# First adapter weights loaded whole and picked on ScalarE, with TensorE's front in another order

## What is computed

```python
def L0(x, lang):                      # all of it per sequence
    h = relu(einsum('bsh,bha->bsa', x, W1[lang]) + b1[lang])      # W1 [10, 128, 32]
    y = x + einsum('bsa,bah->bsh', h, W2[lang]) + b2[lang]
    return layernorm(y) * gamma[lang] + beta[lang]
x = x + L0(x, lang)
# L1: three shared networks and two experts by kind, each relu(x @ wi) @ wo
# with wi [128, 512], wo [512, 128], mixed by a gate that reads token 0
x = x + L1(x, kind)
```

## Time and profile before

| | |
|---|---|
| median of 3 runs | 86.93 us (86.89 to 87.05) |
| the profiled execution | 86.88 us, of which its span is 85.1 |
| TensorE busy | 79.9 us |
| VectorE, ScalarE, GpSimd busy | 62.2, 49.4, 41.1 us |
| granted TensorE clock | 0.999 of full |
| DMA | 11998 packets, 7.49 MB |

### The profile page before, as it was taken

How to read it: one execution, slowest core, us unless ns; L and a number is a source line. 1 busy time by engine, 2 the same in 40 slices (tenths; PEclk the granted TensorE clock), 3 DMA queues, 4 the chain that set the end, 5 groups by cost and what they waited for, 6 DMA issues and landing times.

```text
span 85.1 us, 1653 instructions
## 1 busy us (share of the span) xinstructions
PE 79.9 (94%) x472; PEld 66.5 (78%) x472; DVE 62.2 (73%) x172; ACT 49.4 (58%) x116; POOL 41.1 (48%) x83
## 2 busy tenths in 40 slices
PE   4999999999999999999999899999999999999950
PEld 1377766886788898888999688888999898999820
DVE  4338769999799675446389995459777999389970
ACT  6001096994996699586799364464627555376410
POOL 5950099399439149998667400000001995029800
PEclk9999999999999999999999999999999999999999
DMA  0565746999998293000000000000000000210004
GB/s 1 132 153 146 185 125 158 320 258 344 344 308 258 55 346 113 0 0 8 0 0 0 0 0 0 0 0 0 0 0 8 4 0 0 66 51 18 0 0 123
DMA packets 11998, 7.49 MB, mean 88 GB/s; under 512 B 2358, under 2 KB 10836, under 8 KB 11988
## 3 DMA queue, kind: packets, MB, share of 16 engines
q1 hardware_dynamic: 10784, 6.76, 27.7%
q10 hardware_dynamic: 1076, 0.59, 2.6%
q0 software_dynamic: 128, 0.02, 0.2%
HBM read 5.80 MB, written 0.52 MB: 74 GB/s over the span
## 4 chain that ended last, share of the span: by engine, by line
PE 65%; DVE 12%; POOL 9%; issue 6%; ACT 4%; DVEq 0%; ACTq 0%
PE bank L977 9%; PE bank L957 8%; PE bank L974 8%; PE bank L961 7%; PE bank L958 7%; PE bank L975 7%; DVE hl L749 5%; PE bank L1008 4%; POOL prod L488 3%; ACT hh L552 3%; PE bank L914 2%; PE bank L921 2%; PE bank L1002 2%; PE bank L982 2%; POOL prod L490 2%
## 5 line engine op out<-in xcount | busy, mean ns | idle before, releaser
L749 DVE SCALAR_TENSOR_TENSOR hl<-bank,hh 128x256 fp32r<-128x256 f32 (+2 forms) x60 | 31.5, 526 | 12.4 <-ACT hh L552 11.9
L552 ACT ACTIVATE hh<-bank 128x256 fp32r<-128x256 f32 (+2 forms) x60 | 28.0, 469 | 15.7 <-PE bank L961 15.1
L456 POOL TENSOR_TENSOR wl<-w_raw,wh 128x512 fp32r<-128x512 f32 x17 | 21.7, 1293 | 5.2 <-ACT wh L545 5.2
L977 PE MATMUL bank<-hl,wh 128*128 128x256 f32 (+2 forms) x60 | 20.6, 343 | 0.5 <-DVE hl L749 0.3
L974 PE MATMUL bank<-hh,wh 128*128 128x256 f32 (+2 forms) x60 | 19.8, 330 | 0.0
L975 PE MATMUL bank<-hh,wl 128*128 128x256 f32 (+2 forms) x60 | 19.6, 326 | 0.0
L977 PEld LDWEIGHTS bank<-hl,wh 128*128 128x128 f32 x60 | 11.3, 189 | 3.0 <-DVE hl L749 2.1
L545 ACT ACTIVATE wh<-w_raw 128x512 fp32r<-128x512 f32 x18 | 11.3, 628 | 2.3 <-issue 2.3
L957 PE MATMUL bank<-x1hl,wh 128*128 128x256 f32 (+1 forms) x36 | 12.2, 338 | 0.0
L974 PEld LDWEIGHTS bank<-hh,wh 128*128 128x128 f32 x60 | 11.4, 190 | 0.8
L975 PEld LDWEIGHTS bank<-hh,wl 128*128 128x128 f32 x60 | 11.4, 190 | 0.7
(11 more groups left out here) (111 smaller groups left out, 107.9 us busy)
## 6 DMA issues: line engine op xcount, KB each, us to landing
w_raw<-in_L_cond_expert_wi_dram SPq DMA_DIRECT2D x6, 256.0 KB, 4.4
w_raw<-in_L_cond_expert_wo_dram SPq DMA_DIRECT2D x6, 256.0 KB, 4.7
x_in<-in_x_dram SPq DMA_DIRECT2D x2, 256.0 KB, 3.5
w_raw<-in_L_cond_share_wi_dram SPq DMA_DIRECT2D x2, 256.0 KB, 4.0
w_raw<-in_L_cond_share_wo_dram SPq DMA_DIRECT2D x2, 256.0 KB, 4.2
xs<-x1hl SPq DMA_DIRECT2D x4, 128.0 KB, 4.3
x1hl<-xs SPq DMA_DIRECT2D x4, 128.0 KB, 2.5
out_dram<-o_sb SPq DMA_DIRECT2D x4, 128.0 KB, 1.8
```

The source lines that it names most:

```text
L456: nc.gpsimd.tensor_tensor(wl[:, k, w, :], w_raw[:, k, buf(w), :], wh[:, k, w, :].bitcast(f32), ALU.subtract).then_inc(s_wl[w], 1)
L552: nc.scalar.activation(packed(hh[:, u % NBUF, :], r), packed(h_ps[u % NBUF][:, :], r), ACT.Relu).then_inc(s_hh, 1)
L749: nc.vector.scalar_tensor_tensor(out=packed(hl[:, u % NBUF, :], r), in0=packed(h_ps[u % NBUF][:, :], r), scalar=0.0, in1=packed(hh[:, u % ...
L977: nc.tensor.matmul(dst, wh[:, 1, w, chunk], lo, start=False, stop=(c == FC - 1)).then_inc(s_mm2, 1)
```

## The change

W1 is loaded whole into a new tile W1t, [128, 10, 32], by one DMA on SP that waits for nothing. ScalarE loads all 8 languages into registers and copies each sequence's block from W1t to W1s. SP loads all 8 languages too and issues every load of W2z, and it issues shared set 0 between the halves; W2z's semaphores are now one for each pair. The transposes of half 0 go to two banks, and the copy of xT is divided: pair 0 on VectorE, pair 1 on ScalarE; half 1 is copied by ScalarE, behind its load of the table. The variance plus eps moves from GpSimd to VectorE. VectorE takes `norm_stats(0)` ahead of `window_tables`. TensorE's order in the front changes, with `adapter_out` by pairs; ScalarE's `weights_high(0, 1)` moves behind `x1_high`.

```diff
-        xt_ps = [bank[5], bank[3]]
+        xt_ps = [[bank[5], bank[3]], [bank[3], bank[3]]]
...
-        def load_adapters(engine, h, js):
-            first, last = h * HB + js[0], h * HB + js[-1]
-            langs = loaded(engine, f"lang{first}_", lang_p[0:1, first:last + 1], [L - 1] * len(js))
-            for j, lang in zip(js, langs):
-                engine.dma_start(W1s[:, h * HB + j, :],
-                                 W1[bass.ds(lang, 1), :, :].rearrange("l d a -> (l d) a")).then_inc(s_w1[h], 16)
+        def load_adapters(engine, langs, h):
             engine.wait_ge(s_zero, 1)
-            for j, lang in zip(js, langs):
-                engine.dma_start(W2z[A * j:A * j + A, h, j, :],
-                                 W2[bass.ds(lang, 1), :, :].rearrange("l a d -> (l a) d")).then_inc(s_w2[h], 16)
+            for j in range(HB):
+                engine.dma_start(W2z[A * j:A * j + A, h, j, :], W2[bass.ds(langs[h * HB + j], 1), :, :]
+                                 .rearrange("l a d -> (l a) d")).then_inc(s_w2[(h * HB + j) // PAIR], 16)
...
             sp.dma_start(x_in[:, half(0), :], x[half(0), :, :].rearrange("b s d -> s b d")).then_inc(s_x[0], 16)
+            sp.dma_start(W1t[:, :, :], W1.rearrange("l d a -> d l a")).then_inc(s_w1, 16)
             sp.dma_start(kind_p[:, :], on_all(kind)).then_inc(s_kind, 16)
...
-            load_adapters(sp, 0, (0, 1))
-            load_adapters(sp, 1, range(HB))
+            langs = loaded(sp, "lang", lang_p[0:1, :], [L - 1] * B)
+            load_adapters(sp, langs, 0)
+            load_wi(sp, 0, share_wi[0, :, :])
+            load_wo(sp, 0, share_wo[0, :, :])
+            load_adapters(sp, langs, 1)
...
             def inverse_deviation(n):
-                pool.wait_ge(s_mv, PAIR * (n + 1))
+                pool.wait_ge(s_ve, n + 1)
                 b = slice(n * PAIR, (n + 1) * PAIR)
-                link(nc.gpsimd.tensor_scalar(ve[:, b], mv[:, b, 1], EPS, None, ALU.add))
...
-            load_adapters(act, 0, (2, 3))
-            load_wi(act, 0, share_wi[0, :, :])
-            load_wo(act, 0, share_wo[0, :, :])
+            langs = loaded(act, "lang", lang_p[0:1, :], [L - 1] * B)
+
+            def pick_adapters(h):
+                act.wait_ge(s_w1, 16)
+                for b in range(h * HB, (h + 1) * HB):
+                    nc.scalar.activation(W1s[:, b:b + 1, :], W1t[:, bass.ds(langs[b], 1), :],
+                                         ACT.Copy).then_inc(s_w1c[h], 1)
...
+            pick_adapters(0)
+            act.wait_ge(s_xt, 2)
+            nc.scalar.activation(xT[:, pair(1)], xt_ps[0][1][:, pair(1)], ACT.Copy).then_inc(s_xtc[0], 1)
             adapter_relu(0)
+            pick_adapters(1)
             act.wait_ge(s_tab, 1)
             table = loaded(act, "table", tab_i[0:1, HB:place(SLOTS, 0)],
                            [B - 1] * HB + [B - size(k) for k in range(SLOTS)])
             ranks, starts = dict(zip(range(HB, B), table)), table[HB:]
+            act.wait_ge(s_xt, PAIRS)
+            nc.scalar.activation(xT[:, cols(1)], xt_ps[1][0][:, :], ACT.Copy).then_inc(s_xtc[1], 1)
             weights_high(0, 0)
             add_beta(0)
             adapter_relu(1)
-            weights_high(0, 1)
             x1_high(0)
             x1_high(1)
+            weights_high(0, 1)
+            act.wait_ge(s_xtc[1], 1)
             add_beta(1)
...
                     nc.vector.bn_aggr(mv[:, b, :], stats[:, b, :]).then_inc(s_mv, 1)
+                dve.wait_ge(s_mv, PAIR * (n + 1))
+                b = slice(n * PAIR, (n + 1) * PAIR)
+                nc.vector.tensor_scalar(ve[:, b], mv[:, b, 1], EPS, None, ALU.add).then_inc(s_ve, 1)
...
-            nc.vector.tensor_copy(xT[:, cols(0)], xt_ps[0][:, :]).then_inc(s_xtc, 1)
+            nc.vector.tensor_copy(xT[:, pair(0)], xt_ps[0][0][:, pair(0)]).then_inc(s_xtc[0], 1)
             dve.wait_ge(s_b1p, 1)
             nc.vector.tensor_copy(b1_c[:, :], b1_ps[:, 0:NH]).then_inc(s_b1c, 1)
             sort_by_type()
-            dve.wait_ge(s_xt, 2)
-            nc.vector.tensor_copy(xT[:, cols(1)], xt_ps[1][:, :]).then_inc(s_xtc, 1)
+            norm_stats(0)
             window_tables()
-            norm_stats(0)
             norm_stats(1)
...
             def adapter_in(h):
-                pe.wait_ge(s_xtc, h + 1)
-                pe.wait_ge(s_w1[h], 16 * HB)
+                pe.wait_ge(s_xtc[h], (2, 1)[h])
+                pe.wait_ge(s_w1c[h], HB)
...
             residual(0)
-            residual(1)
-            transpose_x(1)
             adapter_in(0)
             pe.wait_ge(s_par, 16)
             residual_bias(0)
+            adapter_out(0)
+            residual(1)
             residual_bias(1)
-            adapter_out(0)
+            adapter_out(1)
+            transpose_x(1)
...
             transpose_z(0)
             residual(3)
             transpose_z(1)
+            adapter_out(2)
             residual_bias(3)
-            adapter_out(1)
+            adapter_out(3)
```

More of the change, by code:

```diff
@@ L128, in conditional_residual_mlps @@
         kind_p = sb("kind_p", [P, B], i32)
+        W1t = sb("W1t", [P, L, A])
         W1s = sb("W1s", [P, B, A])
@@ L216, in conditional_residual_mlps @@
         s_x = [sem(f"s_x_half{h}") for h in range(NH)]
-        s_w1 = [sem(f"s_w1_half{h}") for h in range(NH)]
-        s_w2 = [sem(f"s_w2_half{h}") for h in range(NH)]
+        s_w1 = sem("s_w1")
+        s_w1c = [sem(f"s_w1c_half{h}") for h in range(NH)]
+        s_w2 = [sem(f"s_w2_pair{n}") for n in range(PAIRS)]
         s_wi = [sem(f"s_wi{w}") for w in range(SETS)]
@@ L233, in conditional_residual_mlps @@
         s_xt = sem("s_xt")
-        s_xtc = sem("s_xtc")
+        s_xtc = [sem(f"s_xtc_half{h}") for h in range(NH)]
+        s_ve = sem("s_ve")
         s_h0 = sem("s_h0")
@@ L515, in _ @@
             act.wait_ge(s_lang, 16)
-            load_adapters(act, 0, (2, 3))
-            load_wi(act, 0, share_wi[0, :, :])
-            load_wo(act, 0, share_wo[0, :, :])
+            langs = loaded(act, "lang", lang_p[0:1, :], [L - 1] * B)
[4 more added lines that the diff above has]
+                                         ACT.Copy).then_inc(s_w1c[h], 1)
             def add_beta(h, js=range(HB)):
                 act.wait_ge(s_colsc, 1)
-                act.wait_ge(s_xtc, h + 1)
+                if h == 0:
+                    act.wait_ge(s_xtc[0], 2)
                 for b in (h * HB + j for j in js):
@@ L882, in transpose_x @@
                 for j in range(HB):
-                    mm = nc.tensor.transpose(xt_ps[h][:, seq(j)], x_in[:, h * HB + j, :], ident[:, :])
-                mm.then_inc(s_xt, 1)
+                    mm = nc.tensor.transpose(xt_ps[h][j // PAIR][:, seq(j)], x_in[:, h * HB + j, :], ident[:, :])
+                    if j % PAIR:
+                        mm.then_inc(s_xt, 1)
             def adapter_in(h):
-                pe.wait_ge(s_xtc, h + 1)
-                pe.wait_ge(s_w1[h], 16 * HB)
+                pe.wait_ge(s_xtc[h], (2, 1)[h])
+                pe.wait_ge(s_w1c[h], HB)
                 if h:
@@ L904, in residual @@
                 if n == 2:
-                    pe.wait_ge(s_xtc, 1)
+                    pe.wait_ge(s_xtc[0], 2)
                 if n == 3:
@@ L915, in residual_bias, with adapter_out @@
                                      start=False, stop=False, skip_group_check=True)
-            def adapter_out(h):
-                pe.wait_ge(s_w2[h], 16 * HB)
+            def adapter_out(n):
+                h, k = divmod(n, 2)
+                pe.wait_ge(s_w2[n], 16 * PAIR)
                 pe.wait_ge(s_h0a, h + 1)
-                for k in range(2):
-                    nc.tensor.matmul(y_ps[2 * h + k][:, pair(0)], ha[:, h, :], W2z[:, h, k * PAIR:(k + 1) * PAIR, :],
-                                     start=False, stop=True, skip_group_check=True).then_inc(s_y, 1)
+                nc.tensor.matmul(y_ps[n][:, pair(0)], ha[:, h, :], W2z[:, h, k * PAIR:(k + 1) * PAIR, :],
+                                 start=False, stop=True, skip_group_check=True).then_inc(s_y, 1)
             def transpose_z(n):
```

## The result

The changed kernel takes 88.02 us (median of 4, 88.00 to 88.05), the kernel before 86.95 beside it: a ratio of 1.0108, 95% interval 1.0071 to 1.0146 (the two medians alone would give 1.0123). Executions that are over 1.5% longer than the others of their kernel are left out of every ratio here, though not of the medians. The forecast was 88.5 and slower; measured are 1.07 us more, forecast were 1.6. The profiled execution took 88.05 with a span of 86.2, against 86.88 and 85.1.

A forecast was written before the change was run, and what follows sets the result against it. TensorE, busy 79.9 of 85.1 us, was taken to bound the kernel, with a tight VectorE chain behind `transpose_z(1)`. The terms 1.2 - 0.1 + 0.5 = 1.6 us on 86.88 gave 88.5, range 87.1 to 89.6.

The forecast's parts named there:

- Weights and picks: Front: W1t lands at 6.0, four picks on ScalarE take 0.7 us, `adapter_in(0)` starts at 7.2 after 0.65 TensorE idle.
- The tables: VectorE's `window_tables`, now behind `norm_stats(0)`: s_tab comes at 10.6 instead of 9.49, 1.1 us later.
- The bare register load: TensorE's `load_starts` behind `adapter_in(1)`, held until 12.5: uncovered for 1.0 us, `transpose_z(0)` at 13.7 instead of 12.5.
- 1.2 - 0.1: Delay of `transpose_z(1)`: `transpose_z(0)` comes at 13.7 instead of 12.5, less the vanishing 0.1 wait, so 1.1 us later.
- The adds: Two more variance adds in VectorE's saturated stretch before `hidden_low(0)`: 2 x 0.25 = 0.5 us (0.2 to 0.6).
- The sum: Whole kernel: 1.2 - 0.1 + 0.5 = 1.6 us on the profiled 86.88, giving 88.5.
- Carried to the end whole: Behind 19.6 us nothing but transfers stands still in time, so the whole 1.6 us reaches the end.
- Slow weights: Rival: W1t goes at the slow packet rate, lands at 7.1 and moves everything by 1.1, giving 89.6; chance 0.12.
- A covered load and weights in time: Rival: weights in time and TensorE's register load short or covered, 87.2 to 87.9; chance together 0.20.
- weights in time, bare load: Case within the 0.20 rival: weights in time, register load bare at 1.0 us, s_tab at 9.9, sum +0.9, 87.8.
- Faster over GpSimd: Rival: the GpSimd path sets `transpose_z(1)`; without its adds z(1) is 0.5 earlier, 86.4, if the load stays covered; chance 0.11.
- No change: Rival: whole kernel, gain and adds cancel, within 0.2% (0.17 us); chance 0.07.

## Why the prediction was right, step by step

**Weights and picks.** Taken: landed 6.0, 0.7 for four picks, `adapter_in(0)` at 7.2, behind 0.65 of idle. Measured: 5.4, 0.59, 6.68, behind 0.33 of idle at its weight loads. The load went faster than the value taken between the two packet rates. The lower bound of 5.6 did not hold either, though it came from the dense row plus x_in's landing. A pick took 213 to 229 ns by itself; the Trainium skill's fit for one (ScalarE: Activation LUTs, What ACT_TABLE_LOAD costs) gives 186 + 0.833 x 32 = 213, and the trace agrees with it. By the Trainium skill's fit for a load (DMA: Bandwidth & Descriptors, Anatomy of one DMA — SWDGE (gpsimd) path), which was measured on loads that GpSimd issues, the 160 KB would take 2.4 us from issue, an estimate. The trace has 3.7 for this one, issued by SP behind 256 KB on the same queue, and the measurement decides.

**The tables.** Taken 10.6, measured 10.13, earlier by what the weights were earlier. The mechanism held: later than 9.49 because of the order on VectorE, and tables first took it away.

**The bare register load.** Taken: `adapter_in(1)` released at 12.5, load 12.65, 1.0 us, `transpose_z(0)` at 13.7. Measured: released 12.02, load 12.1, 1.005 us, 13.35. Right in mechanism (the load moved up, and the load moved down in the kernel before, both show it) and 0.35 to 0.55 too late in its marks. For `transpose_z(1)` the forecast had 1.2 - 0.1, the trace has 0.85 - 0.28 = 0.57. Here both terms of the sum were mis-sized. The first was 0.35 too large because the weights came earlier than taken. The second was 0.18 too small: the 0.1 was read as the gap in front of `transpose_z(1)` between modelled ends, but in the kernel before it starts 0.99 behind `transpose_z(0)`, and in the changed kernel, where nothing waits, 0.71 behind it.

**The adds.** Taken 2 x 0.25 = 0.5 on VectorE. Measured 0.19 and 0.11 for what they cost by themselves, and 0.93 in all in the changed kernel, because one was held for 0.63 us: the stretch that was to take 1.8 us takes 2.26. That hold was in no term, not even in the bounds of 0.2 to 0.6. The profile before could have told: in it `x1_low(0)` had one instruction of 0.41 and one of 0.94.

**The sum.** Forecast 1.2 - 0.1 + 0.5; measured at `hidden_low(0)` 0.22 + 0.93 = 1.15. The first term was too large, and 0.35 us of the delay at `transpose_z(1)` were gone by the statistics, 0.29 of them at `x1_low(0)`, which was no longer held; the last term was too small. The two errors partly cancel, which is luck. "Carried to the end whole" was right: 1.15 at 20.75, 1.17 at the end.

**The rivals.** Slow weights (89.6): no, they came earlier than taken. A covered load and weights in time (87.2 to 87.9): the load wasn't covered; the case "weights in time, bare load" gave 87.8 and is nearest to what was measured. Faster over GpSimd (86.4): its condition, a covered register load, is met in the kernel with the load first, and that one is slower than before still; taking only the adds off GpSimd in the kernel before brought `transpose_z(1)` forward by 0.14, not 0.5, and made that kernel slower too. No change: no.

## What to carry to other kernels

In these runs a register load on TensorE's sequencer was free only while matmuls queued ahead of it were still running, so put it at the earliest point where its table exists, before any wait that may be late. A moved instruction is to be priced beside what the neighbouring engine runs there: look in the trace for the same line with two different durations, and at what GpSimd did during the longer one. A shorter head pays only if every hand-over behind it (here tables, registers, VectorE's order) comes earlier as well: the first statistics came 1.3 us earlier, and the kernel was 1.1 us slower.

## What was not expected of the hardware

- VectorE stood still while GpSimd read two 128x512 weight tiles and wrote a third: an add of 128x2 took 0.80 instead of 0.17 us, a subtraction of 128x256 0.94 instead of 0.41, four additions of 128x128 1.98 instead of 0.89, and an instruction of 128x12 1.27 in the kernel before, against 0.26 with only the weights changed. Beside the same GpSimd instruction, statistics (0.49 us for two), aggregation (0.30), the step that makes x1T with one operand from PSUM (1.22 for four, 1.19 without it) and a one-column add (0.22 for two) were not held.
- The issue of `kind_p`'s load, just behind the one with 1280 packets, took 1.14 us instead of 0.51. With the 0.55 us of the additional issue, the load after it went out 1.2 us later.
- TensorE's clock fell in two profiled executions, those of the kernel with the weights' high part moved back and of the kernel before with the bare load, after the idle time that the register load makes: in the first at its end, in the second some 1.5 us behind it. By stretches of the first of them (us, busy time and count of PE, PEld, DVE, ACT, POOL, then the clock, DMA share, GB/s):

```profile
13.00:14.00 1.00, 0.36 (x6) 0.30 (x3) 0.00 (x0) 1.00 (x5) 1.00 (x1) 0.90 0.43 93
14.00:15.00 1.00, 1.00 (x5) 0.70 (x4) 0.55 (x2) 0.83 (x3) 0.33 (x2) 0.50 1.00 337
15.00:16.00 1.00, 1.00 (x5) 0.76 (x3) 0.40 (x3) 0.42 (x1) 1.00 (x1) 0.50 1.02 280
16.00:17.00 1.00, 1.00 (x4) 0.59 (x3) 0.85 (x4) 0.69 (x3) 0.17 (x1) 0.50 0.68 167
```

  At 0.50, the lower level of 1.2 GHz, for some three microseconds, two matmuls of 128x256 take 1.06 us instead of 0.60, and `hidden_low(0)` is at 19.47, where the second trace of the same kernel has 17.88. That second trace and the one of the changed kernel have 0.63 and 0.64 us of idle at the same place and a clock of 1.00 throughout this stretch. What decides between them stays open.
